# Re-ordering row maximum and exponentials, a shorter expert choice, split matmuls and a bias added once, in a two-layer kernel on one core

## The reference, cut to what matters

```
# layer 0, on xn = _gn(x)
E   = softmax(V_e @ sigmoid(prod + b_e))            # temporal attention, 16x16 a sample
S   = softmax(V_s @ sigmoid(prod2 + b_s))           # spatial attention, 256x256 a sample
out = sum_k einsum(cheb[k]*S, xn) @ Theta[k]        # three graph terms
tc  = conv(relu(out)) + tb ;  res = xn @ rw + rb
y   = relu(res + tc)
x   = x + (y - mean_t(y)) / sqrt(var_t(y) + 1e-5) * gamma + beta     # gamma, beta over t
# layer 1, on _gn(x), token by token
logits = xtok @ gate_w.T ; probs = softmax(logits) ; rw, sel = top_k(probs, 2)
rw = rw / sum(rw)
out = sum over the two chosen experts of rw * ((gelu(x@w1.T) * (x@w3.T)) @ w2.T)
x   = x + out
```

## Time and profile before

| what | value |
|---|---|
| time, median of 3 runs | 695.96 us (695.71 to 696.68) |
| the profiled execution's own time | 695.89 us |
| its span | 694.1 us |
| TensorE matmul busy | 556.2 us (80%) |
| VectorE busy | 402.7 us (58%) |
| ScalarE busy | 242.3 us (35%) |
| GpSimd busy | 217.3 us (31%) |

### The profile page before, as it was taken

How to read it: one execution, slowest core, us unless ns; L and a number is a source line. 1 busy time by engine, 2 the same in 40 slices (tenths; PEclk the granted TensorE clock), 3 DMA queues, 4 the chain that set the end, 5 groups by cost and what they waited for, 6 DMA issues and landing times. The chain is left out here.

```text
span 694.1 us, 11673 instructions
## 1 busy us (share of the span) xinstructions
PE 556.2 (80%) x2488; PEld 363.4 (52%) x2489; DVE 402.7 (58%) x1793; ACT 242.3 (35%) x603; POOL 217.3 (31%) x283
## 2 busy tenths in 40 slices
PE   0567599999999999999982408999999999998243
PEld 0233357766666666766661203666666666665122
DVE  4645226788888888888898552333333333332355
ACT  0343144344444444444431201333333333333232
POOL 5000001224444444444455430344334333434000
PEclk9989599999999999999996556999999999999555
DMA  9900000000000000000000142222222222220796
GB/s 306 415 3 1 1 0 1 0 1 32 31 32 32 31 31 32 32 30 32 32 31 31 49 105 56 90 85 83 81 89 86 83 83 90 89 84 28 219 300 207
DMA packets 36259, 52.84 MB, mean 76 GB/s; under 512 B 4605, under 2 KB 31360, under 8 KB 35968
## 3 DMA queue, kind: packets, MB, share of 16 engines
q1 hardware_dynamic: 24816, 30.86, 14.2%
q0 software_dynamic: 6480, 16.85, 6.6%
q10 hardware_dynamic: 4928, 4.72, 2.1%
HBM read 30.19 MB, written 23.14 MB: 77 GB/s over the span
## 5 line engine op out<-in xcount | busy, mean ns | idle before, releaser
L610 PE MATMUL bank<-w,xT 128*128 x284 | 137.6, 608 | 2.1 <-DVE xT L1399 2.1
L1399 DVE COPY xT<-bank 128x256 f32<-128x256 f32 x71 | 30.2, 425 | 146.9 <-PE bank L597 146.9
L960 POOL DMA_INDIRECT yrows<-xT,dest x71 | 69.4, 977 | 141.4 <-ACT xT L816 135.2
L929 POOL DMA_INDIRECT xrows<-xtok,slot x64 | 67.9, 1061 | 82.1 <-DVEq L1296 67.5
L487 PE MATMUL bank<-work 128*128 128x256 f32 x384 | 93.3, 386 | 0.0
L917 POOL TENSOR_TENSOR yg<-work,sml 128x512 f32<-128x512 f32 x16 | 17.9, 1122 | 187.3 <-DVE work L1206 187.3
L487 PEld LDWEIGHTS bank<-work 128*128 128x128 f32 x384 | 70.4, 190 | 9.0 <-issue 0.8
L625 PE MATMUL bank<-w,xT 128*128 x284 | 73.3, 381 | 1.6 <-ACT xT L821 1.6
L610 PEld LDWEIGHTS bank<-w,xT 128*128 128x128 f32 x284 | 49.3, 194 | 38.2 <-issue 38.2
L810 ACT ACTIVATE xT<-bank 128x256 f32<-128x256 f32 x71 | 27.2, 383 | 98.5 <-PE bank L610 98.5
L625 PEld LDWEIGHTS bank<-w,xT 128*128 128x128 f32 x284 | 48.5, 190 | 6.2 <-issue 2.6
(11 more groups left out here) (201 smaller groups left out, 1020.1 us busy)
## 6 DMA issues: line engine op xcount, KB each, us to landing
xT<-xrows SPq DMA_DIRECT2D x71, 129.0 KB, 2.1
xT<-yrows SPq DMA_DIRECT2D x32, 256.0 KB, 3.9
xs<-x_in SPq DMA_DIRECT2D x4, 1024.0 KB, 11.1
w<-w13t_in SPq DMA_DIRECT2D x1, 4096.0 KB, 18.0
out<-xT ACTq DMA_DIRECT2D x16, 256.0 KB, 3.8
w<-w2t_in SPq DMA_DIRECT2D x1, 2048.0 KB, 22.3
yrows<-xT,dest POOLq DMA_INDIRECT x71, 2.4
xrows<-xtok,slot POOLq DMA_INDIRECT x64, 2.8
```

The costliest lines, as they stand in the source:

```text
L610: last = mm(bank[2 + q][:, :], xc[:, q, c], w13[:, e, c].rearrange("p w n -> p (w n)"), start=(c == 0), stop=(c == C - 1))
L929: pool.indirect_dma_start(xrows, bass.IndirectOffsetOnAxis(ap=slot[:, q, w, k:k + 1], axis=0), xtok[:, q, k], None).then_inc(sc_done[q], 16)
L960: pool.indirect_dma_start(yrows, bass.IndirectOffsetOnAxis(ap=dest[:, q], axis=0), yo[:, q], None, bounds_check=2 * TOKENS - 1, oob_is_err ...
L1399: V.tensor_copy(xc[:, q].rearrange("p c k -> p (c k)"), bank[q][:, 0:C * P]).then_inc(c_xc, 1)
```

## The change

- VectorE and ScalarE order. `row_max` and `recip` no longer have a weave of their own behind the centring and the statistics: they are woven with `ln_a`, `route_a` and `gn_stats`. `ln_b`, `ln_roots` and the choice start in the weave behind it. ScalarE takes `exps` ahead of `square`, and `route_exp` behind `relu`.
- The expert choice works on the shifted logits instead of on probabilities, and takes ten steps in place of eighteen. ScalarE's exponential is of the difference of the two largest only (`r2[:, 4]`); the weights come from it in `route_c`.
- `features` makes four matmuls of 64 rows and 192 columns where there were two of 128 rows and 384 columns. The gate logits are made by four matmuls of 128 columns instead of two of 256, one half of the tokens in rows 0 to 7 and the other in rows 64 to 71, so that one transpose in place of two turns them.
- `beta` is added to all of `xs` once, by 16 ScalarE instructions in the first stage (one for each t, 512 elements a partition at a stride of 16 elements, in place). `ln_out` has two instructions instead of three.

```diff
             def features(b, p, c):
+                pe.wait_ge(s["b_zc"], (b * 4 + c * 2) + START)
                 for h in range(H):
-                    pe.wait_ge(s["b_zc"], (b * 4 + (c * H + h)) + (START - 1))
-                    mm(bank[4 + h][:, 0:K * P], xT[:, b, h, c * P:(c + 1) * P],
-                       thetabd[:].rearrange("p k t o -> p (k t o)"), start=True, stop=True).then_inc(s["b_z"], 1)
+                    for r in range(2):
+                        rows = slice(r * P // 2, (r + 1) * P // 2)
+                        last = mm(bank[4 + r][:, h * K * P // 2:(h + 1) * K * P // 2], xT[rows, b, h, c * P:(c + 1) * P],
+                                  thetabd[rows, :, r * TH // 2:(r + 1) * TH // 2].rearrange("p k t o -> p k (t o)"),
+                                  start=True, stop=True)
...
                 for c in range(C):
-                    last = mm(bank[3][0:E, 0:FT], sm("gate")[:, c * E:(c + 1) * E], xn2[:, c], start=(c == 0),
-                              stop=(c == C - 1))
+                    for k in range(TT):
+                        last = mm(bank[3][64 * k:64 * k + E, 0:P], sm("gate")[:, c * E:(c + 1) * E],
+                                  xn2[:, c, k * P:(k + 1) * P], start=(c == 0), stop=(c == C - 1))
...
+            def add_beta(first, end):
+
+                act.wait_ge(a_xnv, B)
+                act.wait_ge(a_xna, B)
+                for t in range(first, end):
+                    nc.scalar.activation(x_all[:, :, :, t], x_all[:, :, :, t], ACT.Identity,
+                                         bias=sm("beta")[:, t:t + 1], scale=1.0).then_inc(x_beta, 1)
...
             normalise_and_copy(1, 6, GB + 2)
+            add_beta(0, T // 2)
             temporal_tanh(1)
+            add_beta(T // 2, 3 * T // 4)
             temporal_exp(1)
+            add_beta(3 * T // 4, T)
...
             def turn(i, q, ahead2, ahead1, now, back1, back2, back3):
+                if ahead1:
+                    exps(i + 1, 1 - q)
                 if back1:
                     square(i - 1, 1 - q)
-                if back3:
-                    route_exp(i - 3, 1 - q)
-                if ahead1:
-                    exps(i + 1, 1 - q)
...
                 step(nc.gpsimd.tensor_tensor(flat(yg[:]), flat(y[:, p]), over(sm("gamma")), ALU.mult))
-                step(nc.gpsimd.tensor_tensor(flat(yg[:]), flat(yg[:]), over(sm("beta")), ALU.add))
...
                 choice = router(route_b)
-                weave(centre())
-                weave(router(route_a), statistics())
-                variance = layer_norm()
-                weave(attention(), along=(variance, choice))
-                weave(variance, group_norm(), matrices(), choice)
+                weave(centre(), attention(), router(route_a), statistics())
+                weave(layer_norm(), group_norm(), matrices(), choice)
                 weave(router(route_c))
```

More of the change, by code:

```diff
@@ L534, in turn_logits @@
                 pe.nop(nofuse=True)
-                for k in range(TT):
-                    last = nc.tensor.transpose(bank[3][:, FT + k * E:FT + (k + 1) * E], lgT[0:E, k * P:(k + 1) * P],
-                                               cst[0:E, ID:ID + E])
-                last.then_inc(s["b_lg"], 1)
+                nc.tensor.transpose(bank[3][:, FT:FT + 64 + E], lgT[0:64 + E], cst[0:64 + E, ID:ID + 64 + E]
+                                    ).then_inc(s["b_lg"], 1)
             def prefix(b, p):
@@ L745, in copy_features @@
             def copy_features(b, p, c):
[L746 to L748 removed]
+                for r in range(2):
+                    act.wait_ge(s["b_z"], (b * 4 + (c * 2 + r + 1)) + START)
+                    nc.scalar.copy(z[:, p, c, :, :, r * P // 2:(r + 1) * P // 2],
+                                   bank[4 + r][:, 0:K * P].rearrange("p (h k o) -> p k h o", h=H, k=K)
                                    ).then_inc(s["b_zc"], 1)
@@ L786, in turn @@
                     relu(i, q)
+                if back3:
+                    route_exp(i - 3, 1 - q)
                 if ahead1:
@@ L977, in _ @@
             V = nc.vector
-            for n in "b_bs b_max b_rec b_A b_y b_cen b_var b_dn b_st b_q b_nb b_sh b_M b_slot".split():
+            for n in "b_bs b_max b_rec b_A b_y b_cen b_var b_dn b_st b_q b_nb b_sh b_df b_M b_slot".split():
                 dve.sem_inc(s[n], START)
@@ new lines, in route_b @@
+                step = Steps(dve, v_rt2, b, 10)
+                yield from step.then(V.scalar_tensor_tensor(out=rt[:, 4], in0=rt[:, 0], scalar=0.0, in1=row8(cs(DSC, E)),
+                                                            op0=ALU.is_equal, op1=ALU.mult))
+                yield from step.then(V.tensor_reduce(r2[:, 5], rt[:, 4], AX, ALU.max))
+                yield from step.then(V.tensor_tensor(rt[:, 7], rt[:, 4], wide8(r2[:, 5]), ALU.is_equal))
+                yield from step.then(V.scalar_tensor_tensor(out=rt[:, 5], in0=rt[:, 7], scalar=-3e38, in1=rt[:, 0],
+                                                            op0=ALU.mult, op1=ALU.add))
@@ new lines, in route_b @@
+                yield from step.then(V.tensor_reduce(r2[:, 4], rt[:, 5], AX, ALU.max))
+                dve.sem_inc(s["b_df"], 1)
+                V.tensor_scalar(xtok[:, p, :, N + 1], r2[:, 5], -1.0, float(E), ALU.mult, ALU.add)
+                yield from step.then(V.tensor_tensor(rt[:, 3], rt[:, 5], wide8(r2[:, 4]), ALU.is_equal))
+                yield from step.then(V.tensor_tensor(rt[:, 4], rt[:, 3], row8(cs(DSC, E)), ALU.mult))
+                yield from step.then(V.tensor_reduce(r2[:, 6], rt[:, 4], AX, ALU.max))
@@ L1271, in route_b @@
+                yield from step.then(V.tensor_tensor(rt[:, 8], rt[:, 4], wide8(r2[:, 6]), ALU.is_equal))
                 yield from step.then(V.tensor_tensor(mb[:], rt[:, 7], rt[:, 8], ALU.add))
+                step.close()
                 dve.sem_inc(s["b_M"], 1)
-                V.tensor_scalar(xtok[:, p, :, N + 1], r2[:, 5], -1.0, float(E), ALU.mult, ALU.add)
-                yield from step.then(V.tensor_tensor(r2[:, 7], r2[:, 3], r2[:, 4], ALU.add))
-                yield from step.then(V.reciprocal(r2[:, 8], r2[:, 7]))
@@ L1276, in route_b @@
-                wb = wts[:, b]
-                V.tensor_tensor(wb[:, 0], r2[:, 3], r2[:, 8], ALU.mult)
-                yield from step.then(V.tensor_tensor(wb[:, 1], r2[:, 4], r2[:, 8], ALU.mult))
-                step.close()
             def route_c(b, p):
```

45 lines of the change are left out of this document (17 added, 28 removed).

## The result

The changed kernel takes 718.86 us (median of 6 runs: two near 728, four between 718.2 and 719.2) against 694.56 us of the kernel before in the same comparison. The ratio is 1.041, with an interval of 1.037 to 1.0449. It is slower, as forecast, but by 24 us where 10 were forecast, and just outside the range. The profiled execution is one of the two near 728: 728.02 us, span 726.1 us, against a span of 694.1 us before. The four runs near 718 us record a mean granted clock of 0.876 to 0.882, the two near 728 us 0.859 and 0.860; no run near 718 us was profiled.

The account below looks back on a forecast made before the run. One loop through TensorE, VectorE's chain to L1233 and ScalarE's L766 set the 17.87 us turn. Terms: 695.89 + 7 (turns) - 1.8 (features) - 0.8 (late turns) + 5.6 (beta) = 705.9, forecast 706 us, range 684 to 718.

Parts of the forecast that it names:

- TensorE's clock falls: Rival: sparse stretch ahead of the gate matmuls lowers the clock through the logits; +3 us a turn or more, 740; chance 0.08.
- The turn without the clock: Middle stage: a full pipeline turn takes 18.5 us against 17.87, +0.65 a turn, +7 over 11 turns.
- `b_nb` to the row maximum: First part of the turn: from the group norm's `b_nb` through gate matmuls and logits to the row maximum, 4.75 us.
- the tail: End of VectorE's turn: six short instructions behind L1224, held up by GpSimd's two instructions, take 3.55 us.
- Row maximum to L1204: Second part of the turn: VectorE's row maximum to centred `y`, 3.1, then ScalarE's square, 0.7; together 3.8 us.
- L1204 to L1224: Third part of VectorE's turn: two `weigh` and `add_bs`, 37 short instructions and a wait for L515, 6.45 us.
- GpSimd does not hold the new tail: Rival: end of VectorE's turn takes 1.6 us instead of 3.55, turn 16.6, kernel 685 us; chance 0.20.
- No matmuls at the same time: Rival: TensorE's row halves do not overlap, features take 1.39 to 1.5 us, kernel 710 to 716 us; chance 0.16.
- The -1.8: Early turns: split `features` at 0.9 us each save 1 us in about two turns, -1.8 us.
- Beta: End of first stage: ScalarE's 16 additions at 0.95 us spacing delay the chain, +5.6 us.
- The ends: Two late turns: shorter by one GpSimd step of 1.2 us, part taken by other waits, -0.8 us.

Follow-up runs that it names:

- e2_filler: The changed kernel with five extra matmuls a turn whose result nobody reads, four ahead of `prefix` and one behind: 705.95 us, ratio 1.0167.
- e6_pool_later: The changed kernel with GpSimd starting `ln_out` only when the group norm's scale and offset (`b_nb`) are ready: 680.03 us, ratio 0.9828.
- e9_later_spread: The changed kernel with GpSimd's `ln_out` also waiting for `b_nb` and the 16 `beta` additions moved into ScalarE's idle time: 673.47 us, ratio 0.9722.
- e1_old_order: The changed kernel with the old order on VectorE and `square` ahead of `exps` on ScalarE again: 687.33 us, ratio 0.9901.
- e5_beta_spread: The changed kernel with the old VectorE and ScalarE order, and the 16 `beta` additions moved into ScalarE's idle time: 678.84 us, ratio 0.9809.
- e7_best: The changed kernel with the old order, `beta` additions in ScalarE's idle time, and GpSimd's `ln_out` waiting for `b_nb`: 682.65 us, ratio 0.9854.
- e8_splits_only: The kernel before with nothing but the two splits, `features` and the gate logits: 693.36 us, ratio 1.002.
- e4_whole_features: The changed kernel with `features` as before, matmuls of 128 rows and 384 columns in place of row halves: 721.99 us, ratio 1.0427.
- e3_beta_pool: The changed kernel with `beta` added by GpSimd in each `ln_out`, as before, and not by ScalarE: 723.94 us, ratio 1.0442.

## Why the prediction was right or wrong

**The step that failed** is the rival *TensorE's clock falls*: +3 a turn, 740 us, given a chance of 0.08 and left out of the range, with the words "in the rest of the turn TensorE stays dense". So the sum puts the clock at nothing. The clock fell in every full turn, and cost 12.9 us of the medians (e2_filler) and about 20.8 us of the two profiled spans (27.9 over the eleven turns against 7.1 in e2_filler). The place was right (the stretch from the gate matmuls to the logits), and the price too large: the turn is 20.4 us, 1.9 above that of e2_filler instead of 3, since the clock is full again behind the logits and the gate matmuls are slow only in every second turn. That TensorE was dense for the other 17 us did not help. The prediction had named the idle time of 3 us itself, and should have weighed it heavier than the dense rest. The Trainium skill (TensorE: Matmul & The Clock Gate, HAM oscillation — how this bites in real kernels) describes a loop in which the clock falls again in every round because of one wait in it. The changed kernel agrees in that; but the page's wait is longer than the matmuls between, and here 1.76 and 0.84 us of idle time in a turn of 20.4 us were enough, so the page named the danger and does not price this case.

The runs with their idle time, from rows of one typical turn each (us ahead of `prefix`, us ahead of the gate matmuls, and how long the logits took behind it):

| kernel | idle ahead of `prefix` | ahead of the gate | logits | turn |
|---|---|---|---|---|
| before | none | 0.84 | 1.99 | 17.87 |
| e2_filler | none | 0.30 | 1.94 | 18.51 |
| e6_pool_later, e9_later_spread | none | 0.77 | 1.94 | 16.60 |
| e1_old_order | 0.31 | 0.84 | 1.94 | 17.05 |
| e5_beta_spread | 0.31 | 0.84 | 1.94, in one turn 3.59 | 17.06, 18.73 |
| e7_best | none | 0.17 | 1.94 | 17.58 |
| e8_splits_only | 0.87 | 0.84 | 1.94, in four of twelve turns 3.3 to 3.6 | 17.6, 19.3 |
| e4_whole_features | 1.09 | 0.84 | 3.62, twice 1.94 | 20.4, 18.7 |
| changed kernel | 1.76 | 0.84 | 3.25 or 3.71 | 20.4 |
| e3_beta_pool | 2.69 | 0.84 | 2.60 to 3.08 | 20.5 |

**The turn without the clock** was right: 18.52 us in e2_filler against 18.5 (the four parts of the forecast add up to 18.55), and over eleven turns 203.7 us (149.95 to 353.60) against 196.5 before, +7.1 where +7 was forecast. Of its parts `b_nb` to the row maximum (4.75) measured 4.76, and the tail (3.55) 3.53. Row maximum to L1204 was 0.23 too large and L1204 to L1224 0.21 too small. The rival *GpSimd does not hold the new tail* is out, and its price for a turn was exact: with the tail free (e6_pool_later, 1.61 us) the turn is 16.60 where 16.6 was worked out for it; the kernel takes 680.03 us against 685.

**The rest of the sum** came out right by luck. e2_filler, the changed kernel with its clock kept up, takes 705.95 us where 706 was forecast, but only the turns (+7.1) are as forecast: its first gate matmuls come 9.6 us later than before (149.95 against 140.33) where beta and features add up to +3.8, and behind the eleven turns it is 7.2 us shorter (350.1 against 357.3 us) where -0.8 was forecast. The two misses cancel.

The Trainium skill (SBUF — State Buffer, Who interferes with whom) says that VectorE and GpSimd share one pair of ports under an exclusive lock, and that a VectorE instruction with two inputs in SBUF contends with a GpSimd instruction that reads SBUF. The trace agrees in e3_beta_pool, three held instructions in a row, each ending with GpSimd's.

**Features and the other matmuls.** The row halves run together: the call in the earlier trace rows took 1.45 us, and now L451 follows L480 after 0.85 us in the stretch from 263.33 to 264.18. *No matmuls at the same time* is out. The saving shows in the early turns: 13.57 us from 113.74 to 127.31, where the earlier trace rows give 14.25. But the turn ahead of that lost 2.1 us: the clock was at 0.54 from 99.0 to 106.5 us, while in the kernel before it was full from 92.1 us on. The -1.8 came out as about +1.7 (first gate +8.52, of which `beta` 6.82). In e8_splits_only, which has nothing but the splits, the clock is low there too, and from the first copy to the first gate matmuls it takes 60.91 us against 60.14 before; in e9_later_spread, with the clock at 1.00 from 92 us on, 57.38 us. That fits a saving that shows only where the clock stays up, but e9_later_spread differs in more than that. What decides when it comes back at the pipeline's start was not tried.

**Beta.** Forecast +5.6 at a spacing of 0.95; measured +6.8 at 1.05, which is the value "as L678" of the earlier trace rows. Reading at a stride did not cost again on top of that. The size is uncertain by 1 to 2 us: with the same first stage the first copy is at 80.19 us before, 78.92 in e8_splits_only and 77.93 in e3_beta_pool, and with the additions in the queue at 87.01 us in the changed kernel and 86.50 to 88.14 in four other runs.

**The ends.** Forecast -0.8. From the last gate matmuls to the end it is 5.4 us less. 3.1 of these are gone by the first expert's transpose (at 417.48 us before, at 451.79 us in the changed kernel). TensorE's rows show the last `prefix`, of the kernel before, of the changed one and of e8_splits_only:

```profile
401.27 0.17 PE L544 MATMUL bank<-mb,tri 128*128 128x8 bf16 x1 [4.36 <-DVEq L1272]
```

```profile
436.61 0.17 PE L548 MATMUL bank<-mb,tri 128*128 128x8 bf16 x1 [3.29 <-issue]
```

```profile
402.35 0.17 PE L548 MATMUL bank<-mb,tri 128*128 128x8 bf16 x1 [4.31 <-issue]
```

From the gate matmuls to `prefix` it was 7.58 us and is 5.49, 2.1 less. In the last turn almost nothing lies beside the routing, so the splits and the shorter choice both show in full. e8_splits_only, which has the old choice, takes 6.51 us for the same stretch (395.84 to 402.35): the split gate logits are worth 1.07 us of the 2.1, the choice 1.02. The prediction had the choice only among the short instructions of the full turns, where other chains lie between its steps. Of the rest of the 5.4 us no run shows the cause; e8_splits_only has it too, 293.8 us from the last gate matmuls to the end against 300.4 before and 295.0 in the changed kernel.

**What stays open.** In e8_splits_only the clock falls in four of twelve turns, with the same idle time in all; in e5_beta_spread it falls in one; and the changed kernel has runs of 718 and of 728 us of which one of 728 was profiled. Both fit a clock that under the same idle time falls in some turns and not in others; what decides it in the single turn, no run here shows.

## What to carry to other kernels

When a change shortens the dense part of a pipeline's turn or moves a wait into it, ask what TensorE does during the new wait: 2.6 us of idle time in each turn halved its clock for the logits behind it. That cost 13 us of the medians on top of the held tail from which it came (26 us), and filling the idle time with useless matmuls gave the 13 us back. A chain of two-element instructions on VectorE must not be put beside GpSimd's full-tile instructions; one wait that starts GpSimd behind the chain was worth 39 us, but only in the order in which no other work covered the chain. A change with a good and a bad part needs its parts timed apart: the order that looked like the fault was the better one, by 0.45 us a turn, as soon as its tail was free.

## What the runs showed of the hardware that was not expected

- TensorE's clock fell to half in each turn of 20 us, from about 249 to 256 us in one turn and from about 273 to 277 us in the next, with dense work at the full clock between. The dense rest of the turn did not prevent it.
- More idle time did not mean slower logits: with 2.69 us ahead of `prefix` (e3_beta_pool) they take 2.60 to 3.08 us, with 1.76 us (changed kernel) 3.25 to 3.71. In e3_beta_pool the low clock ends inside them.
- A kernel does not have to be slower for more matmuls: 120 matmul records more (2784 instead of 2664), 12.9 us less.
- A VectorE instruction that is held ends within 0.04 us of GpSimd's, so each GpSimd instruction holds one short instruction at most. It is not always the next one: in e6_pool_later L1300 and L1301 start 0.06 and 0.14 us behind L938 and take 0.17 and 0.14 us, and L1302 behind them takes 1.11. In the rows shown here a held one takes 0.84 to 1.23 us instead of 0.16.
- ScalarE's in-place addition of 512 fp32 elements at a stride of 16 elements follows at 1.05 us; one by itself takes 1.13 to 1.23 us (e5_beta_spread). The contiguous square of 512 elements (L760) takes 0.63.
